# VectorE weighs its units of the prior attention in SBUF, and three of every eight in place of two

## The reference, cut to what matters

```python
scores = jnp.einsum('bhqd,bhkd->bhqk', Q, K) * scale            # 16 heads of 16
bias = lam[:, None, None, None] * prior_bias[None, None]        # lam * (0 or -1)
dense_out = jnp.einsum('bhqk,bhkd->bhqd', jax.nn.softmax(scores + bias, axis=-1), V)
s_scores = jnp.where(prior_index_mask[:Ss][None, None], s_scores, -jnp.inf)   # 32 listed keys a query
sparse_out = jnp.einsum('bhsk,bhskd->bhsd', jax.nn.softmax(s_scores, axis=-1), Vg)
out = jnp.where(use_sparse[:, None, None, None], sparse_out, dense_out)
```

## Time and profile before

| what | value |
|---|---|
| median of 3 runs | 1601.97 us (1601.73 to 1603.41) |
| profiled execution, its own time | 1594.84 us |
| its span | 1593.0 us |
| TensorE clock granted, mean | 0.958 of full speed |
| prior attention, first to last exponential | 117.8 to 662.4 us |

### The profile page before, as it was taken

One profiled execution on the slowest core, in us unless ns is written; L12 is line 12 of the kernel. 1 busy time (PEld: TensorE's weight loads), 2 busy tenths in 40 slices (PEclk: granted clock), 3 DMA queues, 4 the chain that ended last, 5 costly groups with the idle time before them and its releaser, 6 DMA issues. The chain is left out here.

```text
span 1593.0 us, 21701 instructions
## 1 busy us (share of the span) xinstructions
PE 1455.9 (91%) x7649; PEld 693.1 (44%) x7697; DVE 1032.9 (65%) x2506; ACT 810.3 (51%) x975; POOL 666.1 (42%) x455
## 2 busy tenths in 40 slices
PE   4788999999999999888998878799999999999988
PEld 2513333332433332333343323345566567777745
DVE  8789878889767886665877493554451437667232
ACT  3753666787556666457765657733332134334101
POOL 5336799998769999613312012141000300000160
PEclk9759999999999999999999979799999999999999
DMA  2340010231311111113242022130000223544061
GB/s 80 122 132 9 27 41 29 89 80 56 80 34 47 38 39 27 35 35 83 91 115 74 21 71 71 55 101 3 1 0 24 93 70 111 177 153 135 28 121 28
DMA packets 74759, 104.52 MB, mean 66 GB/s; under 512 B 14843, under 2 KB 49092, under 8 KB 74650
## 3 DMA queue, kind: packets, MB, share of 16 engines
q1 hardware_dynamic: 70730, 96.66, 20.1%
q0 software_dynamic: 3072, 6.03, 1.9%
q10 hardware_dynamic: 848, 0.43, 0.1%
HBM read 72.39 MB, written 32.77 MB: 66 GB/s over the span
## 5 line engine op out<-in xcount | busy, mean ns | idle before, releaser
L1475 ACT ACTIVATE sb_prob<-wide,sb_ranges 128x1024 f32<-128x1024 f32 (+3 forms) x384 | 380.1, 1006 | 207.8 <-PE wide L2218 114.5
L1249 POOL TENSOR_TENSOR sb_prob<-sb_prob,sb_weight 128x1024 f32<-128x1024 f32 x192 | 448.9, 2363 | 73.1 <-ACT sb_prob L1475 70.9
L2213 PE MATMUL wide<-sb_stack_q,sb_stack_k 114*128 114x512 f16 (+3 forms) x896 | 282.4, 364 | 15.6 <-ACT sb_prob L1475 7.7
L1799 DVE CUSTOM_DVE_ANT_0 sb_junk<-bank,sb_bias 128x512 bf16<-128x512 f32 x345 | 230.4, 687 | 54.0 <-PE bank L2183 49.2
L1522 ACT ACTIVATE sb_sil<-wide,sb_weight 128x320 f32<-128x320 f32 (+1 forms) x128 | 77.5, 607 | 316.0 <-PE wide L2299 259.1
L2183 PE MATMUL bank<-sb_stack_k,sb_stack_q 112*128 112x512 f16 (+3 forms) x601 | 217.2, 378 | 20.5 <-DVE sb_rowmax L1799 5.7
L2233 PE MATMUL wide<-sb_prob,sb_v_aug 128*17 128x512 f32 (+3 forms) x1792 | 223.6, 564 | 10.3 <-ACT sb_o_raw L1487 8.8
L2299 PE MATMUL wide<-sb_weight,sb_ffn 128*128 128x512 f16 x768 | 181.4, 388 | 9.2 <-DVE sb_act_s L2012 7.3
L2012 DVE SCALAR_TENSOR_TENSOR sb_act_s<-wide,sb_weight,sb_sil 128x512 f32<-128x512 f32 x64 | 47.9, 749 | 186.8 <-ACT sb_sil L1522 172.8
L1254 POOL TENSOR_SCALAR_AFFINE_SELECT sb_prob<-sb_prob 128x256 f32<-128x256 f32 x128 | 53.0, 420 | 244.6 <-ACT sb_prob L1475 244.5
L2183 PEld LDWEIGHTS bank<-sb_stack_k,sb_stack_q 112*128 112x128 f16 x601 | 58.8, 98 | 205.4 <-issue 91.3
(11 more groups left out here) (311 smaller groups left out, 1921.2 us busy)
## 6 DMA issues: line engine op xcount, KB each, us to landing
o_raw<-sb_o_raw SPq DMA_DIRECT2D x32, 256.0 KB, 2.2
sb_weight<-rg SPq DMA_DIRECT2D x8, 1024.0 KB, 4.8
sb_xT<-ru SPq DMA_DIRECT2D x8, 1024.0 KB, 4.8
sb_big<-rd SPq DMA_DIRECT2D x8, 1024.0 KB, 6.2
parts<-sb_o_norm SPq DMA_DIRECT2D x40, 128.0 KB
sb_stack_q<-parts SPq DMA_DIRECT2D x32, 128.0 KB, 3.2
sb_stack_k<-parts SPq DMA_DIRECT2D x32, 128.0 KB, 3.2
sb_o_norm<-o_raw SPq DMA_DIRECT2D x64, 64.0 KB, 2.2
```

The costliest lines, as they stand in the source:

```text
L1249: e.tensor_tensor(p, p, weight_of(*u[1:]), ALU.mult).then_inc(weigh_p.handle, 1)
L1475: e.activation(p[:, :, first:HALF], sc[:, :, first:HALF], ACT.Exp, scale=unscale).then_inc(SC.empty_sem(u), 1)
L1799: e.tensor_tensor_reduce(out=junk[:, i % 2, 0:hi - lo], in0=BK.tile(u)[:, 0:hi - lo], in1=bias[:, qt, lo:hi], scale=1.0, scalar=-3e38, op0 ...
L2213: i = e.matmul(sc[:, j * HALF + first:(j + 1) * HALF], stack_k[0:ROWS_M, n % 3, pair, kt * P:(kt + 1) * P], stack_q[0:ROWS_M, n % 3, PAIRS ...
```

## The change

VectorE's units are treated like GpSimd's up to the weighing: ScalarE writes all exponentials into `prob` (the branch that wrote some back into PSUM is gone, and so is its semaphore `exp_a`), and frees the PSUM tile with it. VectorE then caps and multiplies in place in `prob`, so both of its inputs are in SBUF, and tells of it by a semaphore of its own, `weigh_d`; the product with V waits for that. `POOL_UNITS` becomes (0, 1, 3, 4, 6): GpSimd has five of eight units (160 in place of 192), VectorE three, 2, 5 and 7 (96 in place of 64). The second matmuls go with GpSimd's units, so 64 of them fall away. Two waits for the end of the stage ask `weigh_d` in place of `exp_a`.

```diff
-POOL_UNITS = (0, 1, 3, 4, 5, 7)
+POOL_UNITS = (0, 1, 3, 4, 6)
...
-        exp_a = signal("act_exp_wide", [u for u in of("score") if JOBS[u[1]][0] == 0 and not to_pool(*u[1:])])
+        weigh_d = signal("dve_weigh", [u[1:] for u in of("weigh")])
...
-            return weigh_p.after((n, u)) if to_pool(n, u) else SC.emptied(("score", n, u))
+            if JOBS[n][0]:
+                return SC.emptied(("score", n, u))
+            return weigh_p.after((n, u)) if to_pool(n, u) else weigh_d.after((n, u))
...
-                    w.wait_ge(SC.emptied(list(exp_a.value)[-1]))
+                    w.wait_ge(weigh_d.end)
...
-                        w.wait_ge(SC.emptied(list(exp_a.value)[-1]))
+                        w.wait_ge(weigh_d.end)
...
-                    if u in exp_a.value:
-                        e.activation(sc, sc, ACT.Exp, scale=unscale).then_inc(exp_a.handle, 1)
-                        continue
...
-                    w.wait_ge(exp_a.after(key_))
+                    w.wait_ge(SC.emptied(key_))
                     w.wait_ge(weight_ready(n, v))
-                    for mark in prob_vacant((n, v)):
-                        w.wait_ge(mark)
-                    e.scalar_tensor_tensor(out=p, in0=heads_of(SC.tile(key_)[:]), scalar=HUGE, in1=weight_of(n, v),
-                                           op0=ALU.min, op1=ALU.mult).then_inc(SC.empty_sem(key_), 1)
+                    e.scalar_tensor_tensor(out=p, in0=p, scalar=HUGE, in1=weight_of(n, v), op0=ALU.min,
+                                           op1=ALU.mult).then_inc(weigh_d.handle, 1)
```

## The result

| | before | changed |
|---|---|---|
| median of 4 runs each | 1601.85 us (1598.9 to 1603.41) | 1617.07 us (1615.79 to 1621.73) |
| ratio | 1 | 1.0102, 95% interval 1.0077 to 1.0128 |
| profiled execution, its span | 1593.0 us | 1614.4 us |
| prior attention, first exponential of job 1 to that of job 9 | 544.6 us | 561.8 us |

What follows compares the result with a forecast made beforehand. TensorE was taken to set the pace, GpSimd close behind. Each job's longest of TensorE, VectorE and shared SBUF time summed to 599 us against 544.6, 55 more, so a median of 1657 us, range 1608 to 1744.

Steps and rivals of the forecast that it cites:

- 64 second matmuls: TensorE in the prior attention: matmuls that go with GpSimd's units, 0.22 us each, 14.1 us less in all.
- the waits for the PSUM tile: TensorE's weight loads waiting for VectorE's weighing to free the tile: at most 10.7 us saved, some 1.4 a job.
- worked out as 23: Rival with full-size weighings not contending, wait 0: stage 521 us, 23 less, median 1579; chance 0.11.
- w: Wait of each VectorE weighing for GpSimd at SBUF, on top of 1.22 us; taken as 1.2, ends 0 and 2.15.
- The sum: Prior attention, per job the longest of TensorE's, VectorE's and the shared SBUF time, added up: 599 us against 544.6.
- the rule of one instruction: VectorE at SBUF waits for one GpSimd instruction at most: half of 2.36 at 66% load, 0.8 us.
- the orderly turns: Rival: VectorE waits for one GpSimd instruction at most; 26 us more, 1628, or 1610 in step; chance 0.22.
- The 24 weighings of 56.7 us: GpSimd in job 3: 24 weighings of 2.363 us, read as showing GpSimd on TensorE's heels.
- (c): Shared way into SBUF, per job: GpSimd's time less 9.45 plus 12 x 1.22 for VectorE's holds, so + 5.2 us.
- (b): VectorE per job: its busy time before plus 4.9 us plus 12 weighing waits; 19.3 us added at 1.2 each.
- The signs that I named: Expected in the changed profile: weighing mean 2.4 us, VectorE over 90% busy, TensorE waiting for row maxima, stage near 600 us.

Runs made afterwards that it cites:

- before_again: The kernel before, unedited, run once more for a second trace; 1588.82 us in its one run.
- the probe: The kernel before with one small VectorE instruction, both inputs in SBUF, ahead of each of its 64 weighings; 1618.82 us, ratio to before 1.018.
- three_psum: The kernel before with VectorE weighing units 2, 5 and 7 of eight, their exponentials still in PSUM; 1610.51 us, ratio to before 1.0069.
- last_two_halved: The kernel before, VectorE also weighing unit 4 in SBUF in jobs 7 and 8, all GpSimd multiplications cut in two; 1613.91 us, ratio to before 1.0085.

## Why the prediction was right or wrong, point by point

**The mechanism was right.** That VectorE and GpSimd hold each other up where both read SBUF, in both directions, was read from rows 7 to 9 and is shown by the two kernels whose GpSimd only writes. So was who comes late next: row maxima, and TensorE behind them. The work that was to go, 64 second matmuls and the waits for the PSUM tile, went; without contention the kernel gains 26 us, worked out as 23, with the luck named above.

**The step that failed is the size of w.** I took 1.2 us; it measured 0.50. The sum that had given + 54.5 us gives + 11.5 with 0.50, against 15.2 in the medians and 17.2 in the stage. I had its value from L1876, on two grounds that the runs took away. First, I read eight instances as eight samples, and scaled their mean with GpSimd's load. They are one schedule at eight fixed places (before_again), and these are places where GpSimd has a queue; the probe finds 0.60 at a weighing's place in the same schedule, of which I had 64 start times in the trace. What was left of GpSimd's instruction at each gives 0.73, and the same sum with it + 21 us. Second, the 7.18 us had made me set the mean above the 0.8 of the rule of one instruction. For weighings that rule held in every kernel: no wait above 2.2 us beside multiplications of 2.36, none above 1.16 beside halves.

**The rival that came true** is the orderly turns, 1610 to 1630, which I gave 0.22.

**A term that I had too small.** I gave the PSUM tile "at most 10.7 us" from the waits of the kernel before. That is right for two units of eight. For three it is the other side of the change: three_psum shows that taking the third unit in PSUM costs 28.6 us of TensorE's time, and 1.0069/0.9854 or 2.2%, some 35 us, against the same split with no tile held and no contention (there the L1876 are 12 us shorter too, in all). Writing to SBUF buys this back and pays some 40 us for it. The prediction's sum couldn't see that, since it compared with before alone.

**Smaller ones.** The 24 weighings of 56.7 us that I read for job 3 are more than GpSimd's 55.38 there, since its records overlap too: they start 2.33 us apart. (c), the shared way, charged GpSimd the full 1.22 us for each of VectorE's weighings; it was held 0.26 us a multiplication, 42 us of 117. Its extra time nevertheless came out near: in job 8 GpSimd is busy for all of 58.83 us, 62.9 by the sum. (b) took VectorE's busy time as fixed; in the changed kernel the whole stage has 506 us, where 441 + 39 + 48 would be 528. Some 8 us of that are shorter waits of L1876 (10.7 us in all in place of 18.8), and row maxima that follow one another without a gap overlap in the records. These two errors partly cancel the third: that TensorE waits even where no engine is full (67.6 us in job 2, with 63.1, 61.2 and 55.2 busy).

**The signs that I named.** 160 multiplications: right. GpSimd's above 2.363, up to 3.5: right (2.62, 3.37). The weighing's mean 2.4 us with many over 3: wrong (1.72, few), but each that waited ends 1.08 us behind a GpSimd instruction, as named. VectorE busy over 90% of the stage: right, barely (506 of 561.8 us). TensorE waiting for row maxima and no more for the weighing: right. A stage near 600 us: wrong (562). Everything behind it unmoved: nearly.

**Open.** Why an L1876 is sometimes passed over by three or four GpSimd instructions and otherwise gets in at the first end. In the kernel before the one at 580 us missed an end 0.05 us after its start, and the one at 636 us missed ends 0.19, 2.5 and 4.8 us after its start. Both had VectorE idle 0.46 us ahead of them, but so had two in three_psum that got in at the first end, and the four of last_two_halved had not. I have no rule for it.

## What to carry to other kernels

A full-size instruction on VectorE with both inputs in SBUF cost, beside a GpSimd that reads SBUF, what was left of one GpSimd instruction. Price it by the start times of the place where it will stand (0.73 us here, for 0.50 and 0.89 measured), not by another instruction's mean length (1.2), and add what GpSimd is held. How close such instructions stand to each other can matter more than their waits: the same 96 weighings cost 1.0% spread out and 4.5% in threes.

Look for the single long hold before shares and balances. One small instruction that GpSimd's queue passed over stopped TensorE for 5.5 us; a shift of 8 units in two jobs that also removed it gained 0.9%, and a cut of GpSimd's instructions that brought four such holds cost 1.8%.

## What the runs showed of the hardware that I had not expected

The trace repeated from one execution of the kernel before to the next: the stage's VectorE instructions within 0.022 us in length, odd waits included (7.18 and 7.20 us). So a long wait seen once was no chance event. A waiting VectorE weighing always ended at the same distance, 1.08 us, behind the end of one GpSimd instruction. A small VectorE instruction was passed over by three or four GpSimd instructions in a row, once in the kernel before and four times in last_two_halved. A GpSimd multiplication of 128x512 takes 1.27 us where one of 128x1024 takes 2.36.
